# Order of work at the end of the second block's mixer: where GpSimd computes the low parts of the first gated weights, and how far VectorE finishes one half's layer norm before it starts on the other's

## The reference

```python
h = _layernorm(x) * (1 + ca) + sa
x = x + ga * _L1_attn_ref(h, ...)        # the mixer
h = _layernorm(x) * (1 + cb) + sb
x = x + gb * _L1_ffn_ref(h, ...)         # the gated MLP

# end of the mixer
h = xmid + alpha * xmid + (1.0 - alpha) * h
x = x_init + h @ w_up.T + b_up
# the gated MLP; every linear also has a low-rank (LoRA) term
h1 = _lora_linear(x, w1, ...)
h3 = _lora_linear(x, w3, ...)
out = _lora_linear(silu(h1) * h3, w2, ...)
```

## Time and profile before

| | |
|---|---|
| median of 3 runs | 751.21 us (751.1 to 754.94) |
| profiled execution, whole | 754.24 us |
| its span, from the first to the last instruction | 752.4 us |
| TensorE (PE) busy | 709.7 us, 94% |
| VectorE (DVE) busy | 473.2 us, 63% |
| ScalarE (ACT) busy | 318.5 us, 42% |
| GpSimd (POOL) busy | 313.5 us, 42% |
| mean granted TensorE clock | 0.995 of full |

### The profile page before, as it was taken

How to read it: one execution, slowest core, us unless ns; L and a number is a source line. 1 busy time by engine, 2 the same in 40 slices (tenths; PEclk the granted TensorE clock), 3 DMA queues, 4 the chain that set the end, 5 groups by cost and what they waited for, 6 DMA issues and landing times.

```text
span 752.4 us, 10305 instructions
## 1 busy us (share of the span) xinstructions
PE 709.7 (94%) x3742; PEld 432.6 (57%) x3742; DVE 473.2 (63%) x712; ACT 318.5 (42%) x536; POOL 313.5 (42%) x254
## 2 busy tenths in 40 slices
PE   4998899999999999889999999999879999999998
PEld 2444333333333332258787888655548788877886
DVE  3887778788888885237765457758985533338211
ACT  3321357676777767751335401463343223223100
POOL 0335673756565574761446233124522212115300
PEclk9999999999999999999999999999999999999999
DMA  9257516163261200230013100204010111011111
GB/s 322 96 125 222 124 44 165 73 123 57 70 123 26 30 3 24 80 110 18 29 57 98 71 0 1 77 31 86 22 48 1 56 56 55 29 57 58 41 71 42
DMA packets 24111, 53.00 MB, mean 70 GB/s; under 512 B 4252, under 2 KB 8100, under 8 KB 23044
## 3 DMA queue, kind: packets, MB, share of 16 engines
q1 hardware_dynamic: 24068, 52.44, 24.9%
HBM read 45.63 MB, written 6.60 MB: 69 GB/s over the span
## 4 chain that ended last, share of the span: by engine, by line
PE 76%; DVE 13%; issue 4%; DMA 2%; ACT 2%; SPq 1%; POOL 1%; DVEq 0%; ACTq 0%; POOLq 0%
PE ps L866 73%; DVE mxp L1810 3%; DMA rq<-in_mask 1%; DVE st L1652 1%; PE ps L883 1%; DVE xnb L1676 1%; ACT pr L1456 1%; PE ps L1050 1%; DVE rt L1691 1%; DVE x L1894 1%; DVE qsw L1861 1%; PE ps L1118 0%; DVE x L2007 0%; DVE hof L2049 0%; DMA q_parts<-parts 0%
## 5 line engine op out<-in xcount | busy, mean ns | idle before, releaser
L866 PE MATMUL ps<-arena 128*128 128x512 f32 (+1 forms) x1404 | 327.5, 393 | 2.6 <-DVE arena L1695 1.3
L866 PEld LDWEIGHTS ps<-arena 128*128 128x128 f32 (+1 forms) x1404 | 259.9, 186 | 61.4 <-DVE arena L1695 1.9
L1810 DVE TENSOR_REDUCE mxp<-ps 128x2 f32<-128x1024 f32 (+3 forms) x160 | 172.6, 1114 | 42.1 <-PE ps L866 41.4
L1456 ACT ACTIVATE pr<-ps 128x512 f32<-128x512 f32 x288 | 162.1, 596 | 75.1 <-PE ps L866 71.3
L866 PE MATMUL ps<-Qst,Kst 99*128 99x512 bf16 x288 | 99.1, 385 | 6.3 <-ACT pr L1456 5.0
L866 PE MATMUL ps<-Kst,Qst 96*128 96x512 bf16 (+3 forms) x384 | 97.1, 330 | 4.9 <-DVE mxp L1810 4.4
L2242 POOL TENSOR_TENSOR pr<-pr,cap 128x512 int32<-128x512 int32 x56 | 71.1, 1285 | 38.2 <-ACT pr L1456 38.2
L866 PE MATMUL ps<-pr,vr 128*32 128x512 f32 x576 | 76.5, 604 | 0.0
L866 PEld LDWEIGHTS ps<-Qst,Kst 99*128 99x128 bf16 x288 | 24.2, 97 | 79.0 <-ACT pr L1456 63.6
L866 PEld LDWEIGHTS ps<-Kst,Qst 96*128 96x128 bf16 x384 | 35.9, 98 | 50.1 <-DVE mxp L1810 20.8
L2341 POOL TENSOR_TENSOR arena<-raw,arena 128x1024 fp32r<-128x1024 f32 x11 | 26.2, 2390 | 80.4 <-ACT arena L1530 80.4
(11 more groups left out here) (202 smaller groups left out, 837.8 us busy)
## 6 DMA issues: line engine op xcount, KB each, us to landing
wmr<-in_wmr SPq DMA_DIRECT2D x8, 1280.0 KB, 11.2
raw<-in_w SPq DMA_DIRECT2D x16, 512.0 KB, 3.3
Qst<-q_parts SPq DMA_DIRECT2D x42, 128.0 KB
q_parts<-qparts SPq DMA_DIRECT2D x3, 768.0 KB, 5.4
x<-in_x SPq DMA_DIRECT2D x8, 256.0 KB, 6.1
wm<-in_wm SPq DMA_DIRECT2D x4, 512.0 KB, 6.4
raw<-in_up SPq DMA_DIRECT2D x8, 256.0 KB, 2.6
raw<-in_down SPq DMA_DIRECT2D x8, 256.0 KB, 2.6
```

Of the source, the lines that this page charges most:

```text
L866: return nc.tensor.matmul(outp, lhs, rhs, start=start, stop=stop, skip_group_check=True)
L1456: A(pr[:, k % PRING, :], ps[:, 4 + k % 2, :], ACT.Exp, scale=float(DH) ** -0.5).then_inc(exp_done, 1)
L1810: V.tensor_reduce(mxp[:, kh, g0:g0 + heads, i].rearrange("p (b e) -> p b e", e=per), units, AXX, ALU.max)\
```

## The change

It has four parts. (1) GpSimd's low parts of the two weight pieces wait for `ho_ready`, and the second comes behind the first half's `rstd`; its low parts of the first half stand ahead of the second half's `rstd`. (2) VectorE takes the sums of a half only when all four of its tiles are added, normalises its two tiles, adds the next two, finishes the first half's `ln_full`, and only then adds the last two tiles and takes the second half's sums. (3) TensorE does ("F",1) of half 0 ahead of the transposes of half 1. (4) The second half is normalised into a buffer of its own, `xnl`, so that it need not wait for the transposes of the first; ScalarE does ("F",0)'s silu and high part and ("F",1)'s silu ahead of the second half's high parts, and VectorE's `gate_unit` of ("F",0) comes ahead of its `ln_full` of the second half.

```diff
@@ the engines' orders
-             ("up", 0, 1), ("up", 1, 0), ("up", 1, 1)]
+             ("up", 0, 1), ("up_stats", 0, 0), ("norm", 0, 0), ("up", 1, 0), ("full", 0, 0), ("up", 1, 1), ("up_stats", 1, 0)]
 MIXER_POOL = [("out", 0, 0), ("wup", 0, 0), ("out", 0, 1), ("shift", 0, 0), ("shift", 0, 1), ("out", 1, 0),
-              ("out", 1, 1), ("w13", 1, 1)]
+              ("out", 1, 1), ("w13", 0, 0), ("ln", 0, 0), ("w13", 0, 1), ("low", 0, 0), ("ln", 1, 0)]
@@ plan(): banks
-            if (hf, j) == (0, 0):
+            if (hf, j) == (0, 1):
                 turned(3, 1)
@@ tiles
+        xnl = at("xnl", [P, 4, D], F32, ACT_B + 80 * 1024)
+        def normed(L, hf):
+            return xnl if (L, hf) == (3, 1) else xnb
@@ TensorE
             ln_turn(3, 0)
             gated_fresh(("F", 0), ("w13", 0), 0, 0)
+            gated(("F", 1), ("w13", 1), 1, (0,))
             ln_turn(3, 1)
-            gated(("F", 1), ("w13", 1), 1, (0,))
             gated_fresh(("F", 0), ("w13", 0), 0, 1)
@@ ScalarE, ln_norm(hf)
-                filled(act, ("ln", 3, 0, KC - 1) if hf else ("ln", 2, 1, KC - 1))
+                if not hf:
+                    filled(act, ("ln", 2, 1, KC - 1))
@@ ScalarE, the order behind it
             ln_norm(1)
             gate_first(0, ("F", 0), 0)
+            gate_hi(0, ("F", 0), 0, 0)
+            gate_first(0, ("F", 1), 0)
             for c in range(KC):
                 ln_full_hi(3, 1, c, modc[:, 32 + c:33 + c], modc[:, 28 + c:29 + c])
-            gate_hi(0, ("F", 0), 0, 0)
-            gate_unit(0, ("F", 1), 1, (0,))
+            gate_hi(0, ("F", 1), 1, 0)
             gate_unit(0, ("F", 0), 0, (1,))
@@ VectorE
                 elif kind == "up":
                     for t in (4 * y + 2 * hf, 4 * y + 2 * hf + 1):
                         add_x(("wup", t), t, x[:, t, :])
-                        if t % 4:
-                            evacuated(dve, ("wup", t - 1))
-                            ln_stat(y, t % 4 - 1)
-                    if hf: ... ln_stat(y, 3); ln_finish(3, y)
-                    if (y, hf) == (1, 0): ... the two tiles of xnb
-            ln_full(3, 0)
-            ln_full(3, 1)
+                elif kind == "up_stats":
+                    for t in range(4):
+                        evacuated(dve, ("wup", 4 * y + t))
+                        ln_stat(y, t)
+                    ln_finish(3, y)
+                elif kind == "full":
+                    ln_full(3, 0)
+                elif kind == "norm": ... the same two tiles of xnb
@@
             gate_unit(0, ("F", 0), 0, (0,))
+            ln_full(3, 1)
             gate_unit(0, ("F", 1), 1, (0,))
@@ GpSimd
                 elif kind == "w13":
-                    pool.wait_ge(yz_ready, 4 * y + 2 * hf + 2)
-                    for k in range(2):
-                        w13_lo(k, ("w13", k), k)
-            rstd(3, 0)
-            rstd(3, 1)
-            ln_lo_(3, 0)
+                    pool.wait_ge(ho_ready, 4)
+                    w13_lo(hf, ("w13", hf), hf)
+                elif kind == "low":
+                    ln_lo_(3, y)
+                elif kind == "ln":
+                    rstd(3, y)
             ln_lo_(3, 1)
```

More of the change, by code:

```diff
@@ L882, in ln_turn @@
                     for t in range(4):
-                        last = nc.tensor.transpose(ps[:, b, t * P:(t + 1) * P], xnb[:, t, c * P:(c + 1) * P],
+                        last = nc.tensor.transpose(ps[:, b, t * P:(t + 1) * P], normed(L, hf)[:, t, c * P:(c + 1) * P],
                                                    ident[:, :])
@@ L1589, in ln_norm @@
                 act.wait_ge(ln_nb, hf + 1)
-                filled(act, ("ln", 3, 0, KC - 1) if hf else ("ln", 2, 1, KC - 1))
+                if not hf:
+                    filled(act, ("ln", 2, 1, KC - 1))
                 for t in range(4 if hf else 2):
-                    A(xnb[:, t, :], x[:, 4 * hf + t, :], ACT.Identity, scale=rs[:, hf, t:t + 1], bias=nb[:, hf, t:t + 1])\
+                    A(normed(3, hf)[:, t, :], x[:, 4 * hf + t, :], ACT.Identity, scale=rs[:, hf, t:t + 1], bias=nb[:, hf, t:t + 1])\
                         .then_inc(ln_xn, 1)
@@ L2056, in _ @@
                         add_x(("wup", t), t, x[:, t, :])
-                        if t % 4:
-                            evacuated(dve, ("wup", t - 1))
-                            ln_stat(y, t % 4 - 1)
[L2060 to L2069, removed]
-            ln_full(3, 0)
-            ln_full(3, 1)
+                elif kind == "up_stats":
[5 more added lines that the diff above has]
+                    ln_full(3, 0)
+                elif kind == "norm":
+                    dve.wait_ge(ln_nb, 1)
+                    filled(dve, ("ln", 2, 1, KC - 1))
+                    for t in range(2, 4):
+                        V.tensor_scalar(xnb[:, t, :], x[:, t, :], rs[:, 0, t:t + 1], nb[:, 0, t:t + 1], ALU.mult,
+                                        ALU.add).then_inc(ln_xn, 1)
             def gate_unit(i, name, c, halves=(0, 1)):
```

## The result

The changed kernel takes 755.2 us (median of 14 runs, 752.69 to 756.96) against 752.17 us for the kernel before (14 runs, 750.17 to 754.94). The ratio is 1.0039, with a 95% interval of 1.0025 to 1.0053: about 3.0 us slower, between 1.9 and 4.0. The forecast was 751.8 with a range up to 754.5, so the median lies outside. Of the 3.4 us between 755.2 and 751.8, 0.96 is the base alone: the forecast stood on the median of three runs, 751.21, and 14 runs give 752.17. The forecast for the difference was +0.6 us and the measured one is +3.0, still within half a percent of the kernel before.

The account below looks back on a forecast made before the run. TensorE, busy 94% of the span, bounds the kernel. Holes and low clock won (2.28 + 1.28 + 1.98 us) are given back, leaving +0.3 us; 0.3 more for low clock makes +0.6 on 751.21: 751.8 us, range 749.8 to 754.5.

Parts of the forecast that it names:

- the 2.28 + 1.28 + 1.98 us of holes and low clock that go away: TensorE's seam: two holes and a 1.2 GHz stretch vanish, given back as 2.2, 1.4, 1.15 and some 0.6 us.
- +0.3: At the first product of the loop over weight blocks: start 0.3 us later, at 584.4, with TensorE at full clock.
- the low clock of the changed kernel: TensorE between 552 and 567 us: the clock falls again, earlier, and adds 0.3 us.
- the wait at the second transposes: TensorE, free at 566.3 us, waits 1.4 us for the second half's tiles, covering most of the low clock's cost.
- Part 1 frees `hof`: Mixed state's last instruction takes 0.75 us without waiting for GpSimd, ready 2.28 us earlier; rival that it does not: 0.03.
- The costs at nothing beside the first piece: VectorE's additions and sums beside GpSimd's first weight piece cost nothing; at most 2.35 us if they wait.
- VectorE's tiles blocked by the second piece: First half: GpSimd's second weight piece blocks VectorE's two normalised tiles until 552.65 us, so transposes start at 552.7.
- No block: Rival: GpSimd does not block VectorE's two tiles, transposes start at 551.2, total 750.3 us; chance 0.13.
- The hole of 1.28 us closes: TensorE's wait for VectorE's low part of the first half goes; VectorE's low parts end 2.5 us earlier.
- Late next, the second half: VectorE's late sums delay normalisation: TensorE waits 1.4 us, and transposes run from 567.7 to 569.7 us.
- Low clock in the second half: Rivals: one stretch between 568 and 577, 753.5 us, chance 0.14; low through the seam, 756 us, chance 0.08.
- Edits at nothing: Bank order and `xnl` add no instruction; weight loads land 3.3 us later with 20 us to spare.

Follow-up runs that it names:

- b_again2: The kernel before, unchanged, profiled once more: seam 45.25 us, starting at 534.74 us.
- a_again: The changed kernel, unchanged, profiled once more: seam 47.71 us.
- a_warm5: The changed kernel with five added products in TensorE's hole ahead of the first half's transposes: 753.73 us, 1.0027 against the kernel before.
- p1_wait: The kernel before with only GpSimd's two weight pieces made to wait for the mixed state: 750.97 us, 0.9976 against the kernel before.
- a_pieces: The changed kernel with GpSimd's second weight piece moved ahead of the first half's reciprocal root: 754.36 us, 1.0020 against the kernel before.
- b_warm3: The kernel before with three added products in TensorE's hole ahead of the first half's transposes: 753.08 us, 0.9999 against the kernel before.
- p1_late: The kernel before with GpSimd's first piece waiting for the mixed state, the second for VectorE's low parts of the first half: 750.41 us, 0.9981.
- p1_pe: p1_wait plus the change's order on TensorE, ScalarE and VectorE's gates, its bank order and `xnl`: 752.41 us, 0.9997 against the kernel before.
- a_warm: The changed kernel with nine added products in TensorE's hole ahead of the first half's transposes: 755.51 us, 1.0048 against the kernel before.
- p1_late_warm: p1_late with three added products ahead of the first transposes: 749.24 us, 0.9966 against the kernel before.
- b_warm: The kernel before with six added products in TensorE's hole ahead of the first half's transposes: 753.28 us, 1.0011 against the kernel before.

## Why the prediction failed

**The step that failed** is the first half of the sum: "the 2.28 + 1.28 + 1.98 us of holes and low clock that go away". I took the 1.98 us of low clock for a part of the kernel before. In two of its five profiles the low stretch falls on the chain, 24.4 us into the seam, and the seam is 46.8 us. In the other three it falls on the up products or on the transposes and high products, and the seam is 45.2 us. So against most of the executions profiled the kernel before is 1.6 us shorter than the row that I subtracted from, and "+0.3" is +1.9. I had said that the profiled execution is 3.0 us above the median and applied "the difference alone", but the difference was taken from that execution too. It was slow in two places: against b_again2, the fastest profile, by 1.6 us in the seam and by 2.6 ahead of it.

**The term that was mis-sized** is the low clock of the changed kernel: 0.3 us taken, 0.72 in the seam (47.72 against 47.00 with the hole filled, one profile). I had taken the wait at the second transposes to cover nearly all of it. The first transposes took 3.68 us and not 1.97, and the high parts follow them: ScalarE's four took 3.34 instead of 2.79, so VectorE's low parts, its sums and all behind them were later, and a wait of TensorE covers none of that. In a_again TensorE was back at the full clock early enough to wait 1.43 us at the second transposes, and they started at 31.17 us all the same.

Together: 47.7 - 45.2 = 2.5 us in the seam against most executions, 1.8 against the mean of the five (45.88). Measured were 3.0 (1.9 to 4.0). Nothing of it lies behind the seam (168.2 to 168.4 us in all profiles). The remaining 0.5 to 1.2 us would have to lie ahead of it, where no edit was made and executions differ by 4 us; whether they are chance is not shown.

**Point by point**, in us from the start of the first L2049: the forecast's numbers less 537.29, and the profile's less 536.24.

| | forecast | measured |
|---|---|---|
| second L2049 starts | 5.75 | 5.76 |
| `nb` ready | 12.28 | 12.28 |
| VectorE's tiles normalised | 15.36 | 15.32 |
| first transposes start | 15.4 | 15.37 |
| first half's low parts done | 21.6 | 22.37 |
| `nb` of the second half | 27.4 | 28.14 |
| second transposes start | 30.4 | 31.17 |
| ("F",0) of half 1 done | 39.8 | 40.57 |
| loop starts | 47.1 | 47.72 |

The forecast column is the sum at the full clock; 0.3 for the low clock was added behind it, 47.4 in all. With the hole filled and the clock at 1.00 (a_warm5) the loop starts at 47.00.

- *Part 1 frees `hof`*: right (0.75 us), and worth 1.8 us by itself by the ratio of p1_wait, 0.9 in the seam against the short one of before. The costs at nothing beside the first piece were right: four sums took 2.46 us.
- *VectorE's tiles blocked by the second piece*: right, shown by a_pieces, 0.93 us in the seam. "No block" is refuted.
- *The hole of 1.28 us closes*: right.
- *Late next, the second half*: right in place and order. The hole of 1.4 us at the second transposes was there with the clock at 1.00 (1.72, a_warm5) and covered in the longer low stretches, as forecast; the one behind them was 1.14 (1.15 forecast).
- *Low clock in the second half*, once or throughout: in none of three profiles. The low clock came earlier and cost 0.7 us.
- *Edits at nothing* (banks, loads): no wait for either is in the trace.

In short, the sum for the changed kernel was good to 0.1 us at the full clock and to 0.3 us with it, and its waits stood where it had them. But I set it against one profile of the kernel before that had a low stretch on the chain, and took its base from three runs. The comparison of a_warm5 with b_warm3, where the clock is less in play, says the same: 1.0027 against 0.9999, and seams of 47.00 and 45.30. The reordering itself costs; only part 1 of it gains.

## What to carry to other kernels

Before you subtract, ask of each term that a profile shows on the path whether the program causes it or only this execution: a low clock, above all, is to be priced at what most executions pay, which takes several profiles, and a profiled time above the median is a warning. When a wait of one engine for another's running instruction is taken away, look where the instruction that blocked goes next: here it went from one two-input instruction of VectorE to two tiles of it, and the best places found were beside the sums and where GpSimd was idle (p1_late). Products that need nothing new were worth more beside ScalarE's high parts, which otherwise pace TensorE; moved ahead of them they cost 0.7 us of the seam in p1_pe.

## What the hardware showed that I had not expected

- In all six profiles with this order, GpSimd's next instruction got ahead of the VectorE instruction that its last one released: in the changed kernel the piece started at 548.47, before `nb` ended (548.52), and VectorE's two tiles took 3.00 us instead of 1.00. The smallest work is held by a running piece too: a scaling of 128 x 4 numbers took 0.74 us in a_pieces and 1.34 in p1_wait, instead of 0.17.
- The low clock starts at different points of the seam in executions of one kernel (9.6, 10.1, 15.1, 24.4 and 24.5 us into it in the kernel before), and lasts 3.4 us or 6.8. In the profiles of a_warm, a_warm5 and p1_late_warm, with products added in the hole, the clock stayed at 1.00 throughout the seam. In b_warm and b_warm3 it did not: a stretch began in the up products ahead of the added ones.
- A product of 128 x 512 in plain float32 shows as two instructions, 0.88 us in all, against 0.23 for one of the rounded format at the full clock.
